# Moving weight conversions, three DMA queues' work and the last residual addition in an attention and feed-forward kernel

## What is computed

```python
x = x + layernorm(attn(layernorm(x)))        # x: (8, 2048, 4096) f32
x = x + layernorm(ffn(layernorm(x)))
# attn, width 1024, one head over the whole width
qkv = x @ Wqkv + bqkv
p = softmax(q @ k.T / 32)
attn = (p @ v) @ Wo + bo
# ffn, 16 blocks of 256 features of the permuted input
t = gelu(t_block @ up[block])                # 256 -> 1024
out_block = t @ down[block]                  # 1024 -> 256
```

## Time and profile before

| what | value |
|---|---|
| median of 3 runs | 2780.15 us (2776.16 to 2935.38) |
| the profiled execution | 2780.35 us |
| span of its instructions, slowest core (6) | 2778.6 us |
| spans of the 8 cores | 2763.9 to 2778.6 us |
| busy: PE, PEld, DVE, ACT, POOL | 62%, 33%, 21%, 31%, 3% |
| HBM read, written | 287.35 MB, 88.08 MB |

### The profile page before, as it was taken

One profiled execution on the slowest core, in us unless ns is written; L12 is line 12 of the kernel. 1 busy time (PEld: TensorE's weight loads), 2 busy tenths in 40 slices (PEclk: granted clock), 3 DMA queues, 4 the chain that ended last, 5 costly groups with the idle time before them and its releaser, 6 DMA issues. The chain is left out here.

```text
span 2778.6 us, 25443 instructions; the slowest of 8 cores (2763.9 to 2778.6 us)
## 1 busy us (share of the span) xinstructions
PE 1721.5 (62%) x9433; PEld 906.8 (33%) x9600; DVE 578.1 (21%) x1396; ACT 873.7 (31%) x706; POOL 88.7 (3%) x153
## 2 busy tenths in 40 slices
PE   1225999999999100066767676763692791891880
PEld 1223444444444000032323232331351451560550
DVE  4553000000000000024343434343221220221220
ACT  4553000000110000004242333333555655546553
POOL 0000000000002000000000000000000001001001
PEclk7557999999999655578989898987796895995995
DMA  5432323232327998913231313130437546457427
GB/s 92 76 70 43 65 50 65 50 65 50 65 50 95 118 112 106 249 40 60 43 69 35 68 35 68 35 61 34 164 141 233 187 171 222 174 194 223 154 77 242
DMA packets 89287, 287.97 MB, mean 104 GB/s; under 512 B 40128, under 2 KB 52416, under 8 KB 69840
## 3 DMA queue, kind: packets, MB, share of 16 engines
q0 software_dynamic: 16656, 135.32, 29.3%
q1 hardware_dynamic: 72512, 151.01, 15.8%
HBM read 287.35 MB, written 88.08 MB: 135 GB/s over the span
## 5 line engine op out<-in xcount | busy, mean ns | idle before, releaser
L341 PE MATMUL ps_q<-h1T,wbuf 128*128 128x512 bf16 x3010 | 660.4, 379 | 3.4 <-issue 0.2
L341 PEld LDWEIGHTS ps_q<-h1T,wbuf 128*128 128x128 bf16 x3072 | 300.8, 98 | 362.9 <-issue 1.1
L476 PE MATMUL ps_p<-wo_sb,oT 128*128 128x512 bf16 x1002 | 250.5, 412 | 174.9 <-DVE oT L524 173.3
L787 ACT ACTIVATE midT<-ps_m 128x1024 bf16<-128x1024 f32 x256 | 248.9, 1021 | 219.9 <-PE ps_m L904 219.5
L459 PE MATMUL ps_s<-kT,qt 128*128 128x512 bf16 x501 | 115.2, 385 | 278.3 <-DMA qt<-q_scr 277.8
L904 PE MATMUL ps_m<-h2T,up_sb 128*128 128x512 bf16 x968 | 240.7, 380 | 43.6 <-ACT midT L787 35.4
L528 DVE TENSOR_REDUCE negmax<-ps_s 128x1 f32<-128x2048 f32 x16 | 36.5, 2282 | 956.9 <-PE ps_s L459 956.9
L921 PE MATMUL ps_f<-dn_sb,midT 128*128 128x256 bf16 x2048 | 233.4, 273 | 0.0
L921 PEld LDWEIGHTS ps_f<-dn_sb,midT 128*128 128x128 bf16 x2048 | 200.4, 98 | 36.0
L476 PEld LDWEIGHTS ps_p<-wo_sb,oT 128*128 128x128 bf16 x1024 | 106.1, 105 | 318.8 <-issue 218.2
L886 PE MATMUL ps_t<-identG,h 128*128 128x128 bf16 x512 | 44.0, 247 | 234.4 <-ACT h L777 222.5
(11 more groups left out here) (90 smaller groups left out, 1188.2 us busy)
## 6 DMA issues: line engine op xcount, KB each, us to landing
up_sb<-up_bf SPq DMA_DIRECT2D x64, 512.0 KB, 3.7
dn_sb<-dn_bf SPq DMA_DIRECT2D x64, 512.0 KB, 4.6
outb<-x_scr POOLq DMA_DIRECT2D x32, 1024.0 KB, 9.5
out<-outb SPq DMA_DIRECT2D x16, 2048.0 KB, 10.4
xb<-x POOLq DMA_DIRECT2D x16, 1024.0 KB, 8.5
xr<-x POOLq DMA_DIRECT2D x16, 1024.0 KB, 13.2
x_scr<-x1b POOLq DMA_DIRECT2D x16, 1024.0 KB, 6.4
x1c<-x_scr SPq DMA_DIRECT2D x4, 4096.0 KB, 18.8
```

What stands on the lines that cost most here:

```text
L341: last = tn.matmul(ps_q[grp % 4][:], wbuf[fg % 2][:, ct, :], h1T[:, ct, s_i * 512:(s_i + 1) * 512], start=(ct == 0), stop=(ct == CT - 1))
L476: last = tn.matmul(ps_p[pg % 3][:], oT[(t - 1) % 2][:, dt, :], wo_sb[:, dt, cq * 512:(cq + 1) * 512], start=(dt == 0), stop=(dt == 7))
L787: a = s.activation(midT[gi % 2][:, 2 * q:2 * q + 2, :], ps_m[q % 2][:], AF.Gelu)
```

## The change

Five edits. (1) Stage 1 issues no conversions any more; the copy of Wo in DRAM is gone, and stage 2 loads `wo_sb` straight from f32 with a cast on POOL's queue, ahead of `bo_sb`. The conversions of up and down weights are issued in stage 2, two in each token tile, ahead of that tile's `xr` load. (2) SP's queue in stage 2 has the first two q tiles ahead of the v transposes, PE waits for the transposes in groups of four, and SP also stores x1, behind the q load of the same turn. (3) In stage 3 the weight loads go from SP to POOL. (4) The second residual addition is done by DVE, from `x1c`, in place of the accumulating DMAs; SP reloads `x1c` when the chunk's four additions are done. (5) In stage 1 the two scratch tiles are gone: ACT's squares go to the `h1` tile (so its wait for the transposes of two tiles before stands ahead of the squares), and DVE's row sum is a reduction.

```diff
@@ stage 1, POOL @@
-                    for dt in range(8):
-                        d = g.dma_start(out=wo_bf[dt], in_=wo_h[dt])
-                        s_wcw.inc(d, 16)
-                    for gi in range(G):
-                        d = g.dma_start(out=up_bf[gi], in_=up_h[gi])
-                        s_wc.inc(d, 16)
-                        d = g.dma_start(out=dn_bf[gi], in_=dn_h[gi])
-                        s_wc.inc(d, 16)
@@ stage 1, ACT @@
+                            if t >= 2:
+                                s.wait_ge(stp.h, 4 * (t - 1))
                             s.wait_ge(sx[t % 3].h, 16 * (t // 3 + 1))
-                            a = s.activation(vscr[:], xb[t % 3][:], AF.Square,
+                            a = s.activation(h1[t % 2][:], xb[t % 3][:], AF.Square,
                                              accum_out=s2q[:, t:t + 1])
@@ stage 1, DVE @@
-                        a = v.tensor_scalar(out=vscr2[:], in0=xb[t % 3][:],
-                                            scalar1=1.0, scalar2=None,
-                                            op0=ALU.mult, op1=ALU.add,
-                                            accum_out=s1q[:, t:t + 1])
+                        a = v.reduce_sum(s1q[:, t:t + 1], xb[t % 3][:], axis=AX.X)
@@ stage 2, SP @@
-                    sy.wait_ge(s_wcw.h, 128)
-                    for dt in range(8):
-                        d = sy.dma_start(out=wo_sb[:, dt, :], in_=wo_bf[dt])
-                        s_wol.inc(d, 16)
+                    for t in range(2):
...
+                        d = sy.dma_start(out=qt[t % 2][:], in_=src)
+                        sq[t % 2].inc(d, 16)
                     for kt_i in range(T):
...
                         d = sy.dma_start_transpose(v_sb[:, kt_i, :], src)
-                        svt.inc(d, 16)
-                    for t in range(T):
-                        if t >= 2:
-                            sy.wait_ge(s_sc.h, t - 1)
-                            sy.wait_ge(sq[t % 2].h, 16 * (t // 2))
+                        svtg[kt_i // 4].inc(d, 16)
+                    for t in range(2, T):
+                        sy.wait_ge(s_sc.h, t - 1)
+                        sy.wait_ge(sq[t % 2].h, 16 * (t // 2))
...
                         d = sy.dma_start(out=qt[t % 2][:], in_=src)
                         sq[t % 2].inc(d, 16)
+                        j = t - 2
+                        sy.wait_ge(s_x1.h, j + 1)
+                        if j >= 2:
+                            sy.wait_ge(s_x1s[j % 2].h, 16 * (j // 2))
+                        d = sy.dma_start(out=x1_hh[j], in_=x1b[j % 2][:])
+                        s_x1s[j % 2].inc(d, 16)
@@ stage 2, POOL @@
+                    for dt in range(8):
+                        d = g.dma_start(out=wo_sb[:, dt, :], in_=wo_h[dt])
+                        swo.inc(d, 16)
                     d = g.dma_start(out=bo_sb[:], in_=bo_h[:])
                     swo.inc(d, 16)
                     for t in range(T):
+                        for j in (2 * t, 2 * t + 1):
+                            if j < 2 * G:
...
                         if t >= 2:
                             g.wait_ge(s_x1.h, t - 1)
                             g.wait_ge(sxr[t % 2].h, 16 * (t // 2))
                         d = g.dma_start(out=xr[t % 2][:],
                                         in_=x_h[t * 128:(t + 1) * 128, :])
                         sxr[t % 2].inc(d, 16)
-                        if t >= 1:
...
-                            d = g.dma_start(out=x1_hh[j], in_=x1b[j % 2][:])
@@ stage 2, PE @@
-                            if t == 0:
-                                tn.wait_ge(svt.h, svt.n)
...
+                                if t == 0 and kt_i % 4 == 0:
+                                    tn.wait_ge(svtg[kt_i // 4].h, 64)
@@ stage 3, SP @@
+                    for c in range(NF):
                         if c >= 1:
+                            sy.wait_ge(sadd.h, FTS * c)
+                            sy.wait_ge(sxl.h, 16 * c)
...
+                        d = sy.dma_start(out=x1c[:], in_=src)
+                        sxl.inc(d, 16)
+                        for tl in range(FTS):
+                            tg = c * FTS + tl
+                            sy.wait_ge(sadd.h, tg + 1)
+                            if tg >= 2:
+                                sy.wait_ge(sost[tg % 2].h, 16 * (tg // 2))
+                            d = sy.dma_start(out=out_h[tg * 128:(tg + 1) * 128, :],
+                                             in_=outb[tl % 2][:])
@@ stage 3, POOL @@
-                            d = g.dma_start(out=outb[tl % 2][:, 0:2048],
-                                            in_=x1_hh[tg][:, 0:2048],
-                                            accum_op=ALU.add)
...
+                    g.wait_ge(s_wc.h, 32 * 16)
                     for c in range(NF):
+                        for gi in range(G):
+                            gg = c * G + gi
+                            if gg >= 4:
+                                g.wait_ge(sdnt.h, FTS * (gg - 3))
+                                g.wait_ge(swf[gg % 4].h, 32 * (gg // 4))
+                            d = g.dma_start(out=up_sb[gi % 4][:], in_=up_bf[gi])
+                            swf[gg % 4].inc(d, 16)
+                            d = g.dma_start(out=dn_sb[gi % 4][:], in_=dn_bf[gi])
+                            swf[gg % 4].inc(d, 16)
@@ stage 3, DVE @@
+                        for tl in range(FTS):
+                            tg = c * FTS + tl
+                            v.wait_ge(snm4.h, tg + 1)
+                            a = v.tensor_add(outb[tl % 2][:], outb[tl % 2][:],
+                                             x1c[:, tl, :])
+                            sadd.inc(a)
```

127 lines of the change are left out of this document (36 added, 91 removed).

## The result

The changed kernel takes 2641.6 us (median of 10 runs, 2635.1 to 2824.9), the kernel before in the same series 2779.2 us (10 runs, 2775.9 to 2935.4). The ratio is 0.950, with a 95% interval of 0.949 to 0.951: faster by 5.0%. The forecast was 2662, with 2612 to 2727 as its range; the kernel is 20 us faster than that. In single executions, of the kernel before too, one half of the chip or a pair of neighbouring cores finishes late; the ratios leave most of these out, and where a pair was late in a profile I read the other cores.

A forecast was written before the change was run, and what follows sets the result against it. Prediction: three stages with gaps, the longest 277.8 us without PE between projection and attention, from queued weight conversions and stage 2's loads. Terms summed to -118.3 us from the profiled 2780.35, giving 2662 us, range 2612 to 2727.

The forecast's parts named there:

- start of stage 2: End of stage 1: with no conversions queued, stage 2 starts at 921.2 in place of 1107.0, -185.8 us.
- first scores, into the stage: Start of stage 2: q tile 0 lands when POOL's queue runs dry, at 122 us instead of 86.5, +36 us.
- v: Start of stage 2: the v transposes hide behind the softmax and first groups, save about +1 us.
- tiles of stage 2: Token tiles of stage 2: both queues' transfers fit the 33.4 us gap, so 0.
- first x1c load: Start of stage 3: x1c takes turns with the weights on POOL's queue, +7 us.
- three chunk ends (and bodies): Stage 3: x1c is reloaded only after four additions, so h starts late, +16 us each, +48 in all.
- end: Last chunk of stage 3: no reload needed, so the kernel ends at 2754.1 against 2778.6, -24.5 us.
- Stage 1: nothing but its end: Stage 1: the reduction replacing the row sum and the earlier wait of ACT's squares each cost 0.
- 5.1 us each, 30 us for six: Start of stage 2: each conversion queued by POOL takes 5.1 us, so six take 30 us.
- Rival A: Start of stage 2: SP's queue isn't held up, since many small q rows pass per turn; 2622 us, 15%.
- the signs: Listed trace signs if right, among them h about 51 us after the first outb of a chunk end.
- rival C: Stage 3: POOL's queue can't feed the blocks with weights, PE waits 5.2 us per load; +250, 2912 us, 3%.

The follow-up runs named there:

- conv_in_stage1: Changed kernel with the 32 conversions of up and down weights issued at the end of stage 1 again; median 2749.2 us, ratio to before 0.984.
- stage1_as_before: Changed kernel, but stage 1's squares and row sum write to scratch tiles as before the change; 2696.5 us, ratio to before 0.958.
- conv_later: Changed kernel, but no conversion before the third tile's turn in stage 2, then three behind each xr load; median 2621.5 us, ratio 0.945.
- pool_after_v: Changed kernel, but POOL's queue in stage 2 begins with a wait for all v transposes; 2596.5 us, ratio to before 0.934.
- v_one_wait: Changed kernel, but PE waits once for all 16 v transposes ahead of the first attention times v; median 2665.5 us, ratio 0.954.
- both crossed kernels: Changed kernel with the stage 3 of before: 2615.3 us, ratio 0.941; kernel before with the changed stage 3: ratio 1.008 from its two quicker runs.
- the two reload kernels: Changed kernel with x1c reloaded by tile, each reload behind its tile's store: 2599.3 us; with all four reloads behind the first two stores: 2576.2 us.
- weights_on_sp: Changed kernel, but in stage 3 SP issues the weight loads, behind x1c and ahead of the chunk's stores; 2679.3 us, ratio 0.957.

## Why the prediction was right, point by point

The table sets the terms of the forecast beside what the two profiled executions show (us).

| term | forecast | measured |
|---|---|---|
| start of stage 2 | -185.8 | -188.4 |
| first scores, into the stage | +36 | +27.5 |
| v | +1 | 0 |
| tiles of stage 2 | 0 | -2 |
| first x1c load | +7 | +4 |
| three chunk ends (and bodies) | +48 | +46 (-1) |
| end | -24.5 | -23.2 |
| sum | -118.3 | -136.9 |

**Start of stage 2.** Right, with its cause: conv_in_stage1 puts the conversions back and gets the delay back, and in the kernel before the stage waits 35.8 us for POOL's queue alone, when the stores of v have landed. The 2.6 us beyond the forecast are an end of stage 1 that took 3.7 us instead of my 5.5, and PE's end 0.8 earlier. "Stage 1: nothing but its end" was wrong by about 2 us: stage1_as_before gives 1 to 3.5 us back. Which of the three edits it is wasn't tried.

**First scores.** The mechanism held: turns packet by packet, q tile 0 landing as POOL's queue runs dry, and its two tests (27 us from conv_later, 95 from pool_after_v) came out on its side. The size was off, and the mis-sized step is "5.1 us each, 30 us for six", the conversions. Wo and `bo_sb` were complete at 75.5 us (75 forecast), so a cast at 7.3 us was priced well, and the two `xr` took 8.0 each; but the six conversions behind `bo_sb` took 22 us in all, 3.7 each, and the queue was dry at 113.6 us instead of 120. The 5.1 were bytes over time of the conversions of before; the landings there are 4.8 us apart, so that even by them six would take 29. Why they are quicker in the changed kernel is open. The last 2 us of the forecast's 122, from a dry queue to q tile 0, were 0.2.

**Rival A**, that SP's queue isn't held up, is excluded: the counts 788 to 786 and 274 to 273, and 108.5 us for a q tile. Equal counts alone would also come out if each queue passed a bundle of the same size in its turn, but they hold in stretches of 5 us too: 35 to 35 packets from 1010 to 1015 us, on 16 engines, are about two of each queue per engine. The section on queues, rings and completion order in the Trainium skill, DMA: Bandwidth & Descriptors, on which the rival leaned, has an engine drain some 9 to 17 descriptors of a ring before it switches; for these two queues, with a row of q counted as a packet, the measurement decides against that. Its outcome, though, was to be had: pool_after_v gets by a wait what A assumed for free, and the projection 105.3 us into the stage is earlier than A's 120.

**v, and the tiles.** Right. v was late by less than a group's wait hides (v_one_wait: 5.8 us exposed), and the turn of 33.4 us held both queues' bursts. That it was nearly full by my sum (32.7 of 33.4) gave no wait; conv_later, with a third conversion in it, gave none either, so the sum of parts laid end to end was an upper bound here.

**Chunk ends.** That `x1c` is asked for only after the fourth addition, and so +16, is what the trace has: 51.4 us from `outb` to `h`, where the sum gives 36.1 + 16 = 52.1 (the signs said about 51). The addition took 4.42 us as chosen, not 2.3 nor 6.0; the rule on fp32 in the Trainium skill, VectorE: DVE Perf Modes, section on the perf-mode tier table, gives the time here too, with one f32 and one bf16 source. That stage 3 costs what it does is shown by both crossed kernels, and where it comes from by the two reload kernels.

**End, weights.** The span ends 36.8 us behind the start of the last chunk's `outb` (60.0 before), -23.2. No matmul of stage 3 waits for weights from POOL, and the blocks are as far apart as before; rival C is out, and with weights_on_sp the change of queue itself is worth 0 to 8 us at the first load.

The forecast was 18.7 us over the profiled execution (the median is 1.6 below that). 8.5 of them are the first scores, in the main the six conversions, 2.6 stage 1 and its end, 2.9 the first load, 2 and 1.2 the chunk ends and the blocks between them, 1.6 the tiles, 1 the v term; 1.3 at the end go the other way. Nearly all errors have one sign, so no luck of terms that cancel is in the result.

## What to carry to other kernels

When two DMA queues feed one core, count packets, not bytes: a load of small rows finishes only with the backlog of large packets on the other queue. What the next stage needs first, above all if its rows are small, should be landed before the large casts are issued; a wait on the issuing engine cost nothing here and gave 45 us.

Moving an operation from a DMA to an engine changes which buffer is read last. Look at what that read holds: here 4 MB of `x1c` could be reloaded only behind four additions, and this cost more than the freed waits gave, until the reload was cut by tile and put behind the stores for which an engine waits.

A change of many parts should be crossed by stage: two kernels showed that one half gave 163 us and the other took 22 to 26.

## What the runs showed of the hardware that was not expected

- The turns between the two queues stay one to one down to rows of 256 bytes against casts that move 7.4 KB per packet in the one stretch (5.80 MB in 788, against 786) and 10.6 KB in the other (2.90 MB in 274, against 273). I had expected them, but not so exact over so different sizes.
- With the queue to themselves the 16 v transposes took 26 to 28 us of SP's time to issue, beside casts 86 us. The issue time in such a row is in the main that of a full queue, not of the instructions.
- The conversions issued turn by turn cost no time: with two or with three of them in a turn (after, conv_later) the turns are the 44.5 to 46.2 us of before, to 0.2 us. Only the six that stand ahead of the stage's first waits cost something, 27 us of the first scores (conv_later).
- `x1c` took 21.7 us at the chunk ends too, with the weights' queue silent. From 1992 to 2014 us SP's queue alone moved 6.55 MB at 96% of the engines' time: `x1c`'s 4 MB and what was left of the two last stores. It is their data, not another queue, that makes the load longer than the 17.5 us of the earlier trace rows.
